# 64 products of the identity with itself on PE ahead of the first mixing step

## The reference

```
mixed = einsum('bct,bcd->bdt', x, cond_weights[itok_B_0_15])
x     = x + mixed @ W_base.T + b_base + 0.5 * fourier(low-rank update of mixed)
act   = silu(gate(x)) * up(x)                 # 1024 -> 2752, each with an adapter per batch
x     = x + down(act) @ sign(weight).T + bias # 2752 -> 1024 -> 1024
```

## Time and profile before

| | |
|---|---|
| median of three runs | 2058.56 us |
| profiled execution, whole | 2058.98 us |
| its span, first to last instruction | 2057.3 us |
| mean granted TensorE clock | 0.991 |
| PE busy | 2010.0 us (98%), 9320 products and as many weight loads |
| DVE busy | 1476.3 us (72%) |
| ACT busy | 744.1 us (36%) |
| DMA | 217.84 MB, mean 106 GB/s |

### The profile page before, as it was taken

The page is one execution under the profiler, slowest core; times in us unless marked ns, Lnnn a source line. Parts: engine busy times, 40 slices in busy tenths (PEclk is TensorE's granted clock), DMA queues, the critical chain, the costliest instruction groups (busy, mean ns, idle before and its releaser), DMA issues. The chain is left out here.

```text
span 2057.3 us, 33381 instructions
## 1 busy us (share of the span) xinstructions
PE 2010.0 (98%) x9320; PEld 1672.9 (81%) x9320; DVE 1476.3 (72%) x2424; ACT 744.1 (36%) x1394; POOL 518.5 (25%) x900
## 2 busy tenths in 40 slices
PE   6999999999999999999998999999999999999998
PEld 5878888888887888888897788888889778888886
DVE  6578777776758777777666777777756777777774
ACT  3234333332333333333334433333323443333330
POOL 6132222213212222221502222222160232222100
PEclk8999999999999999999999999999999999999999
DMA  9265554542435555554243854444424565544401
GB/s 241 91 134 115 114 114 103 114 99 59 106 88 126 113 114 114 114 114 89 55 130 73 161 111 105 105 104 103 97 62 128 112 137 114 113 103 105 94 21 41
DMA packets 311092, 217.84 MB, mean 106 GB/s; under 512 B 167801, under 2 KB 301817, under 8 KB 311009
## 3 DMA queue, kind: packets, MB, share of 16 engines
q1 hardware_dynamic: 274528, 188.62, 40.1%
q0 software_dynamic: 35328, 24.03, 6.7%
q10 hardware_dynamic: 1152, 4.19, 0.5%
HBM read 203.89 MB, written 12.58 MB: 105 GB/s over the span
## 5 line engine op out<-in xcount | busy, mean ns | idle before, releaser
L1166 PE MATMUL ps<-x,split 128*128 128x512 f32 x1440 | 566.0, 393 | 14.5 <-DVE split L744 10.4
L1168 PE MATMUL ps<-x,split 128*128 128x512 f32 x1440 | 563.0, 391 | 0.0
L1167 PE MATMUL ps<-x,split 128*128 128x512 f32 x1440 | 562.3, 391 | 0.0
L541 ACT ACTIVATE split<-ps 128x512 fp32r<-128x512 f32 x368 | 218.7, 599 | 486.8 <-DVE ps L758 474.2
L1166 PEld LDWEIGHTS ps<-x,split 128*128 128x128 f32 x1440 | 272.1, 189 | 70.2 <-issue 12.2
L446 POOL DMA_DIRECT2D nat_ad<-L_cond_A_down x224 | 137.0, 618 | 724.9 <-DVE ps L758 714.2
L1168 PEld LDWEIGHTS ps<-x,split 128*128 128x128 f32 x1440 | 271.6, 189 | 58.9
L1167 PEld LDWEIGHTS ps<-x,split 128*128 128x128 f32 x1440 | 271.6, 189 | 57.2
L952 DVE TENSOR_TENSOR acc<-ps,acc 128x512 f32<-128x512 f32 x252 | 173.1, 689 | 143.3 <-PE ps L1168 143.3
L1166 PE MATMUL ps<-hidden 128*128 128x512 f32 (+1 forms) x704 | 273.9, 389 | 0.0
L1168 PE MATMUL ps<-hidden 128*128 128x512 f32 (+1 forms) x704 | 273.8, 389 | 0.0
(11 more groups left out here) (110 smaller groups left out, 2679.0 us busy)
## 6 DMA issues: line engine op xcount, KB each, us to landing
nat<-L_cond_W_gate SPq DMA_DIRECT2D x336, 128.0 KB
nat<-L_cond_W_up SPq DMA_DIRECT2D x336, 128.0 KB
nat_down<-L_cond_W_down SPq DMA_DIRECT2D x112, 384.0 KB
nat_a<-L_ffn_weight SPq DMA_DIRECT2D x96, 128.0 KB, 2.7
nat<-effective_weight SPq DMA_DIRECT2D x24, 512.0 KB
nat<-x SPq DMA_DIRECT2D x16, 512.0 KB
nat_b<-L_cond_B_gate POOLq DMA_DIRECT2D x224, 24.0 KB, 2.5
nat_b<-L_cond_B_up POOLq DMA_DIRECT2D x224, 24.0 KB, 2.5
```

Of the source, the lines that this page charges most:

```text
L541: act.activation(dst, src, func).then_inc(piece_hi, 1)
L1166: pe.matmul(dst, a[0], b[0], start=first, stop=False)
L1167: pe.matmul(dst, a[0], b[1], start=False, stop=False)
L1168: return pe.matmul(dst, a[1], b[0], start=False, stop=last)
```

## The change

Ahead of the first mixing step, and behind PE's wait for the constants, PE runs 64 products in which the stationary and the moving operand are both the 128x128 identity in `mix[:, 0, 1, :]`. They go into bank 7: 32 to its columns 0 to 127, then 32 to columns 256 to 383, each with start and stop, so that each overwrites the one before. Nothing reads them, and they raise no semaphore.

```diff
+            def ready():
+
+                for half in range(2):
+                    for k in range(32):
+                        ident = mix[:, 0, 1, :]
+                        pe.matmul(ps[:, 7, 256 * half:256 * half + P], ident, ident, start=True, stop=True)
+
             def low_rank_product():
...
             for semaphore in (down_psum, mixed_psum, up_psum, out_psum):
                 pe.sem_inc(semaphore, START)
+            ready()
             mixing_all(0, making=True)
```

## The result

The kernel got slower: 2062.45 us (median of 16 runs, 2060.82 to 2064.03) against 2057.94 for the kernel before (16 runs, 2055.74 to 2062.22). The difference is 4.5 us by the medians; the ratio, over all runs, is 1.0020, 95% interval [1.0012, 1.0028]. The profiled execution took 2063.54, its span is 2061.9, 4.6 longer than the one shown of before.

A forecast was written before the change was run, and what follows sets the result against it. PE bounds the body (busy 2010.0 of 2057.3 us); only the start has room, carried by DVE behind the first mixing step. Profiled 2058.98 minus 1.0 is 2058.0; against the median 2058.56, 2057.5. Range 2055.3 to 2061.0.

The forecast's parts named there:

- What bounds the kernel, and the products' start: PE bounds the body, DVE the start behind the first mixing step; the added products start at 3.34 us.
- Their pace: Added products ahead of the mixing: the weight load sets the pace, 0.213 us each at half speed, 0.113 at full.
- The bound by the product's own pace: Lower bound for the added products: 46 x 0.11 and 18 x 0.06 us, done at 9.5.
- The clock rose 5.1 us into the mixing: Added products ahead of the mixing: 24 run slowly up to 8.45, 40 take 4.5 us, done at 13.0.
- The upper bound of that same step: Added products at half speed throughout: 64 x 0.213 = 13.6 us, done at 17.0.
- What it gives: 0.98: Full-speed first mixing step removes DVE's 0.98 us idle before its subtraction; all behind moves up; 1.0 taken, 0.5 other end.
- The slower rival: Added products do not raise the clock; mixing starts 2.5 us late and still slow: 2061.1 us, chance 0.11.
- its deciding point: Added products delay the mixing from 0.174 us a product on; below that they are through by 14.46.
- the sentence on identity products in transpose mode: Skill page: identity products in transpose mode do not count as clock activity; by that the slower rival would hold.
- The rival that the clock falls again ahead of the mixing: PE idles after the added products, clock back at half at 14.46: no gain, 2058.6 us, chance 0.22.
- The rival of the later falls: The half-speed stretch from 125.6 us and two like it in later groups vanish: gain 1.0 + 4.5, 2053.1 us, chance 0.05.

The follow-up runs named there:

- dense numbers: The change with a 128x128 corner of x (random normal numbers, one load and one cast more) instead of the identity: 2063.2 us, ratio to before 1.0026.
- the wide products: The change with two identities side by side as moving operand, 256 columns instead of 128, still 64 products: 2057.89 us, ratio to before 1.0004.
- all of it: Kernel before plus 64 products of 256 columns ahead of mixing, 10 ahead of its fifth step, 14 before the first weight tile, 3 behind half tiles: 2064.04 us.

## Why the prediction was wrong

*What bounds the kernel, and the products' start:* right in kind. They began at 3.8 and not 3.34: the loads begin 0.56 behind DVE's cast and not 0.14.

*Their pace:* right. I took the load as what sets it and 0.213 at half speed; it was 0.214. The bound by the product's own pace, done at 9.5, does not hold in a stream of loads. The Trainium skill, page "TensorE: Matmul & The Clock Gate", section "Back-to-back issue gap", gives N/1.2 ns for an isolated product at half speed and says that this leaves the loads out; by it 128 such products would take 13.7 us (estimate), and the trace shows 27.3.

*"The clock rose 5.1 us into the mixing ...; with the same delay 24 products run slowly, ... and 40 take 4.5 us: done at 13.0."* This is the step that failed. It took a rise measured under the mixing's products, of 256, 128 and 256 columns, for products of 128 columns alone. The runs put something else in its place: 64 and 128 products of 128 columns, of zeros and ones or of random numbers, ran at half speed for 13.7 and 27.3 us without a rise, and under 64 of 256 columns the clock rose after 3.0. Nor is 5.1 a constant under the mixing itself: in the change its loads came at full speed 3.1 us after its start (17.49 to 20.59), with dense numbers 5.9 (18.10 to 23.97). Why products of 128 columns alone don't bring the rise stays open. The upper bound of that same step, done at 17.0, was the outcome, 17.49.

*"What it gives: 0.98"*: not reached in the change, as the mixing started late and at half speed. Where the mixing did start at full speed, the traces bear this part out: 0.74 won up to the weight tiles with the wide products and 1.1 with all of it, and a wait of 1.40 ahead of the fifth step, where I had said 1.3. The time with the wide products stayed that of before: the 1.0 would have been below what the measurement tells.

*The slower rival* was the right one in its mechanism, its deciding point (0.174 us a product, 0.214 measured) and the end of the products (17.0, 17.49 measured). Its reason was wrong: I tied it to the zeros of the identity, and random numbers do the same. So the sentence on identity products in transpose mode named the outcome but not its cause; these were plain products and the identity plays no part. Its price was too low, 2.5 against 4.5, and the term that was mis-sized is the start of the mixing without the products: I took the 14.46 of one profile, the latest of twelve. With the average of DVE's twelve starts, 12.55, and 0.44 behind it, that start is 13.0, and the products delay the mixing to 17.49 by 4.5 (estimate), as much as was measured. The tile stage, 1.9 longer in the profile of the change, is no second term that the runs show: with dense numbers it took 11.42 behind a mixing as late, at no less time, and the kernel before alone gave 11.69 and 12.62. The end of the range, 2061.0, stood on that sum.

*The rival that the clock falls again ahead of the mixing* does not apply, since there was no rise. The rival of the later falls is not what moved the time: between the two profiles the difference is 4.66 at 115 us and 4.57 at the last product's reader (DVE L995, 2048.04 to 2052.61).

Of the wait ahead of the first step nothing but its end was read: it is a load whose arrival varies by 2.7 us between profiles (ACT behind it at 10.94 to 13.68), and a filler sized against its latest arrival is too long for the others.

## What to carry to other kernels

Filler (products that nobody reads) that is to raise PE's clock should be of a form that was seen to raise it in the kernel at hand, with the same columns behind each load; PE busy for the whole time is no evidence. Ahead of work that waits for a transfer, size filler by the earliest arrival and at the slow pace, for if the clock does not come, all of it stands in the way, a microsecond for a microsecond. The same holds for filler inside a stage: it must fit at the slow pace too, or one fall of the clock makes it the bound.

## What was not expected of the hardware

PE can be busy without a break for 27.3 us and stay at 1.2 GHz (128 products of 128 columns, 0.213 us each). The zeros of the identity made no difference to that: 416 ns a product with the identity and with random numbers. The column of the granted clock reads 1.00 from the start of a profile to its first change, while the spacing of products shows half speed (3.8 to 6.7 us with the wide products, 0.213 each): at the start the spacing has to be read.

With wide products ahead of the mixing and around the tiles together, one new wait of 3.2 us, put down to issue, stood ahead of the second group's products at 604.5 us while the wait for the adapters' input there was gone; how the added instructions bring that about was not tried. In the two of twelve runs with five products behind each half tile that were 10 us above the others, the mean granted clock was 0.989 and not 0.995; with three products, where the clock fell in the tile stage, it is 0.989 to 0.990 in all six. That it fell there in those two runs as well is likely but not shown, as no profile of them exists.
